# A two-layer decoder on one core: the stages of two threads in one merged order instead of in turn

## What is computed

```
x = layernorm(x + gated_linear_attention(x))      # layer 0: 4 heads, keys 64, values 128
x = layernorm(x + cross_attention(x, context))    # 16 heads of 16
x = layernorm(x + experts(x))                     # 8 experts, top 2, hidden 512
x = layernorm(x + window_attention(x))            # layer 1: 16 heads of 16, window +-128
x = layernorm(x + cross_attention_clipped(x, context))
x = layernorm(x + experts_with_capacity(x))       # 8 experts, top 2, hidden 256
```

## Time and profile before

| | |
|---|---|
| median of 3 executions | 1343.07 us (1342.0 to 1349.29) |
| the profiled execution | 1350.57 us, span 1348.6 us |
| TensorE busy | 1047.2 us, 78% of the span |
| VectorE busy | 574.5 us, 43% |
| ScalarE busy | 365.8 us, 27% |
| GpSimd busy | 248.8 us, 18% |
| granted TensorE clock, mean | 0.848 of full speed |
| attention part of layer 0 | 10 to 386 us |
| dispatch and experts of layer 0 | 386 to 677 us |
| attention part of layer 1 | 687 to 1202 us |
| dispatch and experts of layer 1, end | 1202 to 1348.6 us |

### The profile page before, as it was taken

How to read it: one execution, slowest core, us unless ns; L and a number is a source line. 1 busy time by engine, 2 the same in 40 slices (tenths; PEclk the granted TensorE clock), 3 DMA queues, 4 the chain that set the end, 5 groups by cost and what they waited for, 6 DMA issues and landing times.

```text
span 1348.6 us, 19033 instructions
## 1 busy us (share of the span) xinstructions
PE 1047.2 (78%) x7654; PEld 704.3 (52%) x7655; DVE 574.5 (43%) x1230; ACT 365.8 (27%) x495; POOL 248.8 (18%) x300
## 2 busy tenths in 40 slices
PE   6989889899830899999947978888797869754910
PEld 3756756666520466566644646565564646443600
DVE  2545435525450122222237346455735482642216
ACT  2344234244310122222112331414053204311200
POOL 0302201202127000000050103011210107002056
PEclk9889888898865899999968869877996879666965
DMA  5010100500058411111120001000100002013786
GB/s 155 1 36 0 35 2 0 162 27 1 1 190 308 110 43 43 47 44 42 43 74 1 5 2 32 1 5 0 32 2 4 1 0 95 1 39 108 204 89 121
DMA packets 61174, 71.08 MB, mean 53 GB/s; under 512 B 12320, under 2 KB 51248, under 8 KB 61104
## 3 DMA queue, kind: packets, MB, share of 16 engines
q1 hardware_dynamic: 51168, 50.80, 12.1%
q0 software_dynamic: 6144, 16.79, 5.8%
q10 hardware_dynamic: 3792, 2.48, 0.7%
HBM read 46.18 MB, written 23.86 MB: 52 GB/s over the span
## 4 chain that ended last, share of the span: by engine, by line
PE 56%; DVE 20%; POOL 10%; ACT 5%; issue 4%; DMA 4%; SPq 1%; POOLq 0%; DVEq 0%; ACTq 0%
PE ps L1490 9%; PE ps L1218 7%; DVE sb_arena L699 5%; PE ps L1338 5%; PE ps L1404 5%; PE ps L1314 4%; POOL rows_in L1116 4%; PE ps L1504 4%; DVE sb_arena L703 3%; ACT sb_arena L522 3%; PE ps L1455 2%; PE ps L1360 2%; DVE ps L729 2%; POOL sb_arena L1176 2%; PE ps L1346 2%
## 5 line engine op out<-in xcount | busy, mean ns | idle before, releaser
L1490 PE MATMUL ps<-sb_arena 128*128 x312 | 149.8, 604 | 1.3 <-issue 0.3
L522 ACT ACTIVATE sb_arena<-ps 128x2048 f32<-128x2048 f32 (+2 forms) x80 | 121.0, 1533 | 55.6 <-PE ps L1296 40.0
L1218 PE MATMUL ps<-sb_arena,sb_wreg 128*128 128x256 f32 (+2 forms) x512 | 119.7, 378 | 4.2 <-issue 3.5
L1218 PEld LDWEIGHTS ps<-sb_arena,sb_wreg 128*128 128x128 f32 (+1 forms) x512 | 95.8, 200 | 25.1 <-issue 7.9
L1087 POOL TENSOR_TENSOR sb_arena<-sb_arena,sb_eps 128x2 f32<-128x2 f32 x48 | 11.7, 243 | 526.5 <-DVE sb_arena L665 526.4
L1314 PE MATMUL ps<-sb_arena 32*77 32x256 f32 (+1 forms) x1024 | 95.9, 510 | 4.5 <-ACT sb_arena L522 2.9
L986 DVE TENSOR_TENSOR sb_arena<-ps,sb_arena 128x512 f32<-128x512 f32 x39 | 27.0, 692 | 145.3 <-PE ps L1490 111.3
L1490 PEld LDWEIGHTS ps<-sb_arena 128*128 128x128 f32 x312 | 56.4, 193 | 46.1 <-issue 44.7
L735 DVE RECIPROCAL sb_arena<-ps 128x32 f32<-128x32 f32 x24 | 8.6, 358 | 167.3 <-PE ps L1346 166.1
L1116 POOL DMA_INDIRECT rows_in<-sb_xres,sb_scat x64 | 62.1, 970 | 93.6 <-DVE sb_scat L947 60.8
L1123 POOL DMA_INDIRECT sb_arena<-rows_out,sb_gath x32 | 30.7, 959 | 249.3 <-DMA rows_out<-sb_arena 240.3
(11 more groups left out here) (206 smaller groups left out, 1762.5 us busy)
## 6 DMA issues: line engine op xcount, KB each, us to landing
sb_arena<-in_m_w SPq DMA_DIRECT2D x24, 512.0 KB, 12.0
rows_in<-sb_zeros SPq DMA_DIRECT2D x1, 4992.0 KB, 17.3
sb_arena<-rows_in SPq DMA_DIRECT2D x39, 128.0 KB, 2.1
rows_out<-sb_arena SPq DMA_DIRECT2D x39, 128.0 KB, 1.7
sb_arena<-in_m_w SPq DMA_DIRECT2D x16, 256.0 KB, 2.9
sb_arena<-rows_in SPq DMA_DIRECT2D x8, 384.0 KB, 4.6
rows_out<-sb_arena SPq DMA_DIRECT2D x8, 384.0 KB, 3.6
sb_arena<-in_xT SPq DMA_DIRECT2D x8, 256.0 KB, 3.1
```

Source lines behind the costliest of these rows:

```text
L522: nc.scalar.activation(dst, src, ACT.Exp).then_inc(S(f"h_PT{p}"), 1)
L1218: ins = mm(dst[:, m * cols:(m + 1) * cols], wt[0:rows[k], k, m * P:(m + 1) * P], src[0:rows[k], k, 0:cols], start=(k == 0), stop=(k == KC ...
L1490: ins = mm(bank(p, a), slots0[p].xT[:, k, :], weights0(e, a * KC * FH + k * FH, FH), start=(k == 0), stop=(k == KC - 1))
```

## The change

Each thread gets a list of its own, in the order that it had before, and a function merges the two. Each stage is given a length in TAKES (1 where it has no entry); the stages of thread 0 start at 0 and those of thread 1 at LAG = 12, each starts where the one before it in its thread ends, and the merged list is sorted by these starts. The unit is a rough microsecond; by it a pair lasts 99 in the first layer and 119 in the second. choose, count and early now belong to thread 1's list, so count uses bank 7 instead of bank 3 and waits for thread 1's values, and the wait for the copied counts moves to thread 1's first scores.

```diff
-def lockstep(n, stages):
-
-    return [(s, p, n) for s in stages for p in range(2)]
+TAKES = {"g_keys": 4.5, "g_sp": 3.5, "g_wv": 3.5, "g_sums": 3, "g_dec": 1.5, "g_wg": 3.5, "g_th": 2, "g_scal": 2, "g_sc": 1.5, "g_mask": 2,
+         "g_mix": 2.7, "g_y": 2.5, "g_rms": 2.5, "g_nd": 1.7, "g_wo": 3.5, "k": 1.8, "q": 1.8, "v": 1.8, "scores": 1.7, "max": 2.2,
+         "split": 1.5, "nmT": 0.5, "nmTe": 0.5, "ST": 2, "exp": 2, "clip": 1.3, "shift": 0.3, "values": 2.5, "wo": 1.8, "mix": 3,
+         "res": 2, "g_res": 2, "xb": 0, "store": 0}
+
+LAG = 12
 def first_layer():
-    out = lockstep(0, [("g_keys",), ("g_low",), ("g_decay",), ("g_z",)])
+    head = [("g_keys",), ("g_low",), ("g_decay",), ("g_z",)]
+    out = [(s, 0) for s in head]
     for n in range(PAIRS):
...
+        ahead = [(s, n + 1) for s in head] if n + 1 < PAIRS else []
+        out += ahead[:2] + [(("o_turn",), n), (("o_T",), n)] + ahead[2:] + [(("o_route",), n), (("o_logits",), n), (("store",), n)]
     return out
-def second_layer(n):
...
+def second_layer(p):
+
+    mix = [("mix",), ("mix_rstd",), ("mix_fin",)]
+    out = [(s, 0) for s in mix + self_head(S1)]
+    for n in range(PAIRS):
+        for s in self_stages(S1, [("between",)]):
+            if s != ("between",):
+                out.append((s, n))
+            elif n + 1 < PAIRS:
+                out += [(s, n + 1) for s in mix]
+            elif p == 1:
+                out.append((("early",), n))
+        out += [(s, n) for s in cross_stages(X1, True)]
+        ahead = [(s, n + 1) for s in self_head(S1)] if n + 1 < PAIRS else []
+        out += ahead[:2] + [(("o_turn",), n), (("o_T",), n)] + ahead[2:3] + [(("o_route",), n), (("o_logits",), n), (("store",), n)] + ahead[3:]
+        if n + 2 == PAIRS and p == 1:
+            out += [(("choose",), n + 1), (("count",), n + 1)]
     return out
+
+
+def interleaved(threads):
+
+    timed = []
+    for p, stages in enumerate(threads):
+        at = LAG * p
+        for k, (stage, n) in enumerate(stages):
+            timed.append((at, p, k, (stage, p, n)))
+            at += TAKES.get(stage[0], 1)
+    return [what for _, _, _, what in sorted(timed, key=lambda x: x[:3])]
...
-        order0 = first_layer()
-        order1 = [second_layer(n) for n in range(PAIRS)]
-        head1 = lockstep(0, [("mix",), ("mix_rstd",), ("mix_fin",)] + self_head(S1))
+        order0 = interleaved([first_layer() for p in range(2)])
+        order1 = interleaved([second_layer(p) for p in range(2)])
...
-                v.tensor_copy(counts[:, :], bank(0, 3)[:, 0:2 * P]).then_inc(S("counts"), 1)
+                v.tensor_copy(counts[:, :], bank(1, 3)[:, 0:2 * P]).then_inc(S("counts"), 1)
...
-                    if c is S1 and n + 1 == PAIRS and p == 0:
+                    if c is S1 and n + 1 == PAIRS and p == 1:
                         pe.wait_ge(S("counts"), 1)
...
-                pe.wait_ge(S("h_va0"), S1.at(n) + 1)
-                count(2, 3)
+                pe.wait_ge(S("h_va1"), S1.at(n) + 1)
+                count(2, 7)
```

More of the change, by code:

```diff
@@ L153, in first_layer @@
-    return out
-def second_layer(n):
-    ahead = [(("mix",), p, n + 1) for p in range(2)] + [(("mix_rstd",), p, n + 1) for p in range(2)] \
-        + [(("mix_fin",), p, n + 1) for p in range(2)]
-    out = []
-    for s in self_stages(S1, [("between",)]):
-        if s == ("between",):
-            out += ahead if n + 1 < PAIRS else [(("early",), 0, n)]
-        else:
-            out += lockstep(n, [s])
-    out += lockstep(n, cross_stages(X1, True))
-    if n + 1 < PAIRS:
-        out += lockstep(n + 1, self_head(S1)[:2])
-        out.append((("k", S1), 0, n + 1))
-        out += lockstep(n, [("o_turn",), ("o_T",)])
-        out.append((("k", S1), 1, n + 1))
-        out += lockstep(n, [("o_route",), ("o_logits",), ("store",)])
-        out += lockstep(n + 1, self_head(S1)[3:])
-        if n + 2 == PAIRS:
-            out += [(("choose",), 0, n + 1), (("count",), 0, n + 1)]
-    else:
-        out += lockstep(n, [("o_turn",), ("o_T",), ("o_route",), ("o_logits",), ("store",)])
-    return out
+        stages = [(s,) for s in ("g_sp", "g_wv", "g_vs", "g_sums", "g_dec", "g_wg", "g_th", "g_scal", "g_gate", "g_gw",
+                                 "g_sc", "g_mask", "g_mix", "g_sq", "g_y", "g_rms", "g_nd")]
@@ new lines, in first_layer @@
+        stages += [("k", X0), ("g_turn",), ("g_yT",), ("g_wo",), ("g_res",), ("g_rstd",), ("g_fin",)] + cross_stages(X0, False)[1:]
+        out += [(s, n) for s in stages]
+        ahead = [(s, n + 1) for s in head] if n + 1 < PAIRS else []
+        out += ahead[:2] + [(("o_turn",), n), (("o_T",), n)] + ahead[2:] + [(("o_route",), n), (("o_logits",), n), (("store",), n)]
+    return out
+def second_layer(p):
[14 more added lines that the diff above has]
+            out += [(("choose",), n + 1), (("count",), n + 1)]
+    return out
@@ L617, in _ @@
             act.wait_ge(S("rescaled"), 3)
-            play(head1, stages)
-            for order in order1:
-                play(order, second)
+            play(order1, second)
             router(2)
@@ L1027, in dispatch_early @@
                 dispatch1(0, EARLY)
-            play(head1, stages)
-            for order in order1:
-                play(order, stages | {"choose": choose_early, "count": count_early, "early": dispatch_early})
+            play(order1, stages | {"choose": choose_early, "count": count_early, "early": dispatch_early})
             choices(2 * PAIRS)
@@ L1165, in _ @@
                 gather_choice(p, 0, 1, TILES0 * P)
-            play(head1, stages)
-            for order in order1:
-                play(order, stages | {"store": lambda p, n: store(p, n, X1),
-                                      "early": lambda p, n: scatter(4, 2 * B - 2, 0, EARLY)})
+            play(order1, stages | {"store": lambda p, n: store(p, n, X1),
+                                   "early": lambda p, n: scatter(4, 2 * B - 2, 0, EARLY)})
             scatter(5, 2 * B, EARLY, TILES)
@@ L1542, in count_early @@
             def count_early(p, n):
-                pe.wait_ge(S("h_va0"), S1.at(n) + 1)
-                count(2, 3)
-            play(head1, stages)
-            for order in order1:
-                play(order, stages | {"o_turn": lambda p, n: turn_result(p, n, X1),
-                                      "o_route": lambda p, n: route(p, n + PAIRS, r1), "count": count_early})
+                pe.wait_ge(S("h_va1"), S1.at(n) + 1)
+                count(2, 7)
+            play(order1, stages | {"o_turn": lambda p, n: turn_result(p, n, X1),
+                                   "o_route": lambda p, n: route(p, n + PAIRS, r1), "count": count_early})
             def turn1(p, h):
```

10 lines of the change are left out of this document (removed).

## The result

The kernel after takes 1542.99 us (median of 4, 1534.31 to 1546.54) against 1342.53 on the same chip: 1.147 times as long, interval 1.141 to 1.153, or +200 us. The forecast was 1433, range 1365 to 1487. The sign was right; the forecast rise of 90 us is less than half of what came.

A forecast was written before the change was run, and what follows sets the result against it. TensorE, busy 78% of the span, looked like the bound, with losses to small waits and half clock. First layer +20, second +12 and clock +58 made +90 us, 1441 on the profiled execution, forecast as 1433, range 1365 to 1487.

The forecast's parts named there:

- (a): First layer: thread 1's scores wait for its gate, queued behind thread 0's y on VectorE; 6.35 us of TensorE idle.
- (b): First layer: transpose of thread 1's normed heads waits 1.15 us for the norm, thread 0's output product 1.1 for yT.
- (i): Second layer: VectorE takes the next pair's mix 0 before thread 1's fourth maximum; nmT 1 waits 3.35 us, then 0.4.
- (l): Second layer, clipped cross-attention: two threads out of step give sixteen waits of 0.1 to 1.65 us, 13.3 in all.
- (k): Second layer: thread 1's exp 1 precedes OT 0 on ScalarE; untr 0 waits 3.0 us, wo 0 and values 1 2.0, 1.95.
- the scatter's stop: Second layer's last pair: TensorE stops for 10 us because thread 0's rstd stands behind the early scatter issues on GpSimd.
- (d): First layer: TensorE waits for exponentials of 1.87 us; idle 0.8, 0.8 and 0.75 us.
- (g): Second layer: thread 0's head and first scores against thread 1's projections; idle only 1.1, 0.5, 0.5 us, called good merging.
- The clock: Both layers: half-clock stretches cost 4.5 and 10 us a pair, +58 us in all; bounds 0 to 8 and 20.
- The clock holds: Rival, whole kernel: waits as walked but no added half clock; 1375 us, range 1350 to 1395, chance 0.2.
- faster: Rival, both layers: one thread's projections fill the other's waits, idle halved at full clock; 1281 us, chance 0.08.
- Worse: Rival: half clock through both attention stages of each layer, beyond the clock bound of 112 us; over 1487 us, chance 0.06.

The follow-up runs named there:

- the second run: The kernel after, unchanged, run again on the chip of the experiments: 1554.38 against 1376.04 us, 1.128 times the kernel before.
- scal_first: The kernel after with thread 1's scalars and gate ahead of thread 0's y in layer 0: 1528.83 us, 1.109 times the kernel before.
- l0_merged: The kernel before with the merged order in layer 0 alone: 1462.04 against 1378.09 us, 1.058.
- filler: The kernel after with 14 unread matmuls behind thread 0's mix in layer 0, no stage moved: 1561.57 us, 1.135 times the kernel before.
- The filler in layer 0: The kernel after with 7 unread matmuls behind thread 0's mix in layer 0: 1545.84 us, 1.123 times the kernel before.
- the fillers in layer 1: The kernel after with unread matmuls in two self-attention waits, three before thread 0's untranspose, two before its output product: 1553.92 us, 1.126 times the kernel before.
- l1_moves: The kernel after with three moves in layer 1's self-attention lists (maximum and split, OT, onT moved earlier): 1536.17 us, 1.113 times the kernel before.
- lag0: The kernel after with LAG = 0 in place of 12, giving stage by stage in turn again: 1.008 times the kernel before.

## Why the prediction was wrong

**The waits were right.** Nearly all had their place, their releaser and their length: (a) 6.98 for 6.35; (b) 1.18 and 1.11 for 1.15 and 1.1; (c) 0.93 and 1.56 for 0.95 and 1.4; (e) 1.86 and 1.97 for 1.95 and 1.9; (h) 2.96 and 2.39 for 2.8 and 2.3; (i) 3.18 for 3.35; (j) 1.97 twice for 2.05 and 2.0; (l) 13.3 in a window that has 15.0 idle (1013.2 to 1078.7, below); (k) 2.88, 2.02 and 1.97 for 3.0, 2.0 and 1.95; the scatter's stop 12.23 for 10. The small ones were less exact: (d) 1.1 us twice for 0.8, (g) 0.73, 0.66 and 0.66 for 1.1, 0.5 and 0.5. The sums are 20.7 for 19.35 and 37.4 for 35.65. In the second run single waits differ ((i) is 1.60), and the sum of a pair of layer 1 is 36.3. All signs that the prediction listed came, and none of them could tell 1433 from 1543. That the 6.98 at L1426 are list order and can be had back was shown by scal_first.

**The step that failed is the term "The clock", 4.5 and 10 us a pair.** Busy time less the walk's work, from one end of thread 1's values to the next: 87.0 to 91.5 less 77.35, and 112.8 less 89.1, so 10 to 14 and 23.7 us. Both are over my upper bounds of 8 and 20 as well. By the same count the kernel before has 82.2 to 83.1 less 77.35, so 5 to 6 us, and 104.7 less 89.1 = 15.6. The term thus had TensorE lose less to the clock than before, with twice the idle time. The reason I gave, that part of a stretched matmul hides in another engine's wait, was not borne out where it can be read: the slow L1426 stands behind a wait and is itself waited for (VectorE L798, 14.7 us in four pairs).

Where the rest is, by landmark (end of thread 1's values), all in us:

| | walked with its clock | measured | over |
|---|---|---|---|
| layer 0, first landmark | 107.8 | 118.1 | 10 |
| three pairs | 3 x 101.2 | 111.5, 107.7, 112.3 | 28 |
| end of layer 0 | 12.6 | 19.9 | 7 |
| layer 1, mix to first landmark | 138.4 | 154.6 | 16 |
| two pairs | 2 x 134.75 | 150.2, 150.1 | 31 |
| last pair | 146.75 | 152.8 | 6 |
| end of layer 1 | 12.6 | 19.4 | 7 |

Together 105, and 3 less at the experts and the end, so the 102 between 90 and the 192 by which the spans differ. (The first landmarks are those before, 94.3 and 120.4, plus the walk's 9 and 8 and the clock.) In the steady pairs 85 to 90% of the excess is busy time; the ends, walked at full clock although one thread alone leaves TensorE idle four tenths of the time, ran at 0.50 and 0.59. In the two first parts TensorE is busy 11.8 and 16.4 us longer than in the kernel before and idle 12.3 and 18.0 us longer; the walk gives no such split for them.

**Where the half clock is.** The share of a stretch at 1.2 GHz is twice what its mean clock lacks. Windows of one pair of layer 1, first the kernel before, self-attention with the head and then cross-attention with the end; below them the kernel after:

```profile
821.80:888.00 66.20, 57.56 (x624) 39.78 (x623) 35.85 (x67) 20.96 (x20) 13.04 (x18) 0.95 0.06 17
888.00:944.80 56.80, 47.20 (x397) 31.20 (x396) 29.65 (x58) 17.33 (x24) 6.85 (x10) 0.70 0.02 3
```

```profile
928.50:1013.20 84.70, 62.29 (x610) 42.35 (x608) 38.39 (x70) 21.02 (x21) 14.58 (x19) 0.86 0.05 14
1013.20:1078.70 65.50, 50.52 (x414) 32.42 (x410) 28.75 (x55) 16.59 (x23) 4.89 (x7) 0.71 0.01 3
```

Half clock in the first part: 0.05 x 2 x 66.2 = 7 us before, 0.14 x 2 x 84.7 = 24 after. In the second: 34 and 38. In this run, then, the cross-attention, on which the prediction leaned ("the cross-attention, with waits of the same kind, was at half clock"), changed little, and the self-attention, which had kept 2.4 GHz, lost part of it. The split is not the same in every execution: the second run of the kernel after has 17 and 45 us, and on the chips of the experiments the old order (l0_merged) has 11 and 34. The sum is steadier, 41 and 45 us in the old order, 62 in both runs of the new one. I had looked for today's slow stretches to last, and not for fast ones to become slow.

The Trainium skill, "TensorE: Matmul & The Clock Gate", "Part 1: The HAM clock gate", has half rate as the default that activity lifts. The fillers bear that out: matmuls whose result is never read keep 1.00 where 0.50 stood (344 to 417 in filler). As cited, the rule does not say how much half clock the stalls bring; the number that failed was my own.

**The rivals.** "The clock holds" (1375) and "faster" (1281) fell with the first windows; the waits they needed gone were there. "Worse", over 1487 by half clock through both attention stages, had 0.06 and is nearest: half clock in layer 1's pair is 60 of 150 us, in layer 0's 28 of 109, not through all of it. The range ended at 1487 because the bound of 112 us ended there, and the clock went past that bound without this rival's condition.

**What stays open.** How much of the loss the clock alone makes cannot be given as one number. The filler in layer 0 brought back 3.7 us a pair on average, the fillers in layer 1 nothing, the moved stages between 0 and 11 for 6.5 us of idle. In the kernel after twice the idle time came with about twice the clock's loss in layer 0 (5 to 6 us before, 10 to 14 after) and one and a half times in layer 1 (15.6 and 23.7), but idle time alone does not give the loss. With LAG = 24 the pair of layer 1 shown above is idle for 25.0 us against 18.3 in the kernel before, and its loss is 101.0 less 89.1 = 11.9 us, less than the 15.6; two pairs of l1_moves are both idle for 34 us and lose 17 and 23. So which waits make the half clock is shown for the one at L1426 and, by the fillers, for the splits of the kernel before; for the others it is argued. The half clock of the clipped cross-attention (34 us a pair before, 38 and 45 in the two runs after, with the pair's end) was not tried.

## What to carry to other kernels

Here two threads that took the engines in strict turn covered each other's short waits; the list sorted by estimated times put one thread's short step behind the other's long one, and since each engine plays its list in order, the other engines waited too. Walk the list by hand: it gave most waits to a few tenths. Then do not price the clock under today's loss when the idle time doubles, as I did, and keep the range wide: the loss per pair was 10 to 14 and 24 us here, but 12 to 14 in layer 1 at LAG = 24. Look for the stretches at full clock that the new waits may break. Where a wait is fixed and a bank is free, try matmuls that nobody reads, no longer than the wait, and compare two executions before reading anything into one slow place.

## What the hardware showed that was not expected

- Two or three matmuls in a wait, whose result nobody reads, made the kernel before faster by 1.6% (0.984), with 85 us at full clock where it had fallen behind the split.
- A filled wait does not always pay: in layer 1 of the kernel after the matmuls behind it took 1.99 us each time, and the whole time stayed the same (1.126 against 1.128).
- Where the half clock stands differs between two executions of one program: the same untranspose at the end of a pair takes 1.09 us in one and 1.97 in the other, while the pair takes 150.2 and 150.3.
- The same program is 2.5% longer on the chips of the experiments (1376 to 1379 for 1343), most of it in one pair: while the early scatter runs, TensorE has idle pieces of up to 2.4 us put down to issue (lag0), and the pair takes 158 or 159 us for 131. In the merged order VectorE waits 34 us there during the scatters, which it does not on the first chip. The cause was not looked for, nor whether it is the chip.
